# A graph network and expert kernel on one core: the transfers that clear the experts' input leave the first adjacency blocks and come at every fourth block from number 50 on

## The chip, the cores and the metric

The program runs on one core of a Trainium2 chip. The core has TensorE (PE in the rows), VectorE (DVE), ScalarE (ACT), GpSimd (POOL) and SyncE (SP). SyncE computes nothing here: it issues transfers, one after the other, in the order of its program, and waits in that order too. The metric is the device time of one execution in microseconds; lower is better.

## The reference, cut to what matters

A layer norm, four relational graph layers over 3125 nodes of width 256 and 100000 edges of four types, and a mixture of eight experts of which each node takes two:

```python
cnt = zeros((3125, 4)).at[dst, etype].add(1.0)
inv_deg = 1.0 / maximum(cnt[dst, etype], 1.0)
for l in range(4):
    h = einsum('ni,rio->rno', X, W[l])
    agg = segment_sum(h[etype, src] * inv_deg[:, None], dst)
    out = agg + X @ root[l] + bias[l]
    X = elu(layernorm(out) * gamma[l] + beta[l]) + X
...
top_vals, top_idx = top_k(xn @ Wr + br, 2);  w = softmax(top_vals)
y = sum over e of w_full[e] * (gelu(xn @ W1[e] + b1[e]) @ W2[e] + b2[e])
```

The edges are sorted by destination, and low destinations have many more edges than high ones.

## The kernel before, in words

The 3125 nodes are 25 tiles of 125. In layer 0 the first 12 tiles, numbered 0 to 11 ("dense" tiles), get an adjacency matrix: each tile is built in 25 blocks of five destination nodes, 300 blocks in all. A block is summed on TensorE (`pair`, L1859, from one-hot operands that VectorE makes at L1495 and L1500 and ScalarE at L1277 and L1280), and ScalarE copies it out (L1296). When a tile's 25 blocks stand, SyncE issues the tile's count row (L1145, a small transfer within the chip's memories called n_tabs<-n_BIG, on which TensorE's degree matmul L1833 waits) and the store of the whole tile to HBM, 3.1 MB (L1147, n_a<-n_BIG), to be read again in layers 1 to 3. The other 13 tiles ("far" tiles, 12 to 24) take their edges' rows by gathers that GpSimd issues (L1421), twelve of them ahead, and small matmuls (L1907); in layer 0 their edges are counted by L1845.

For each tile the counts become inverses on VectorE (L1515, L1517). They take a round trip: SyncE stores them (L1153, n_ind<-n_INVA, two transfers), waits for that store, and loads them back spread over all partitions (L1119, n_INVB<-n_ind). The end of a tile's sum (`finish`, L1601) multiplies by them and so waits for that load. Behind it come the transposes (L1772), the products with the layer's weights (L1923, L1927), and the norm on VectorE (L1627 and on).

The experts' input is a buffer n_xg in HBM of 25728 rows of 1028 bytes. It must be zero before the routing scatters rows into it, after layer 3. It is cleared by 54 transfers of 96 x 5 rows (L1212, n_xg<-n_tabs, the last one 96 x 3), 26.4 MB in all, issued by SyncE with no wait of their own but for the constants. Two places wait for all of them: the first ScalarE copy of layer 1's sums (L1309, step `fh` with i == T), which overwrites the zeros' source, and the first scatter (L1434).

One list, `order`, sets the work of all engines. `Near.steps` simulates the engines with fixed costs and appends steps; each engine's program walks the list and takes the steps that are its own. A `zx` step is one clearing transfer, and only SyncE takes it. `N_ZERO` is 54, `GPT` is 25 blocks to a tile. A second program for other inputs (`dense_scalar`, `dense_tensor` and more) stands behind a branch on a flag; with these inputs it is not taken, and the rows show none of its lines.

Of the kernel before, what the change touches and what calls it, by code (L numbers as in the profile page):

```python
# [24 lines left out]
GPT = TN // GD  # L25
# [19 lines left out]
BATCH = 4  # L45
# [4 lines left out]
ZROWS = 96  # L50
ZN = 5
N_ZERO = math.ceil((DUMMY + 128) / ZROWS / ZN)
ROWS = (0, 112), (112, TN)
HEAD = 32
SIGMA = 4.0
# [21 lines left out]
S8 = 8  # L77
# [42 lines left out]
class Near:  # L120
# [102 lines left out]
    def steps(self):  # L223


        TD, T_ = self.TD, T
        order = self.order = []
# [44 lines left out]
        def follow(what, l, n):  # L272
            if what == "wscale" and time["pe"] < begun[l]:
                later(time["pe"] + 0.5, what, l, n)
                return
            if what == "weights":
                load_weights(l)
                return
            if what in ROUTE:
                route(what, n)  # L280
                return
            order.append((what, l, n))
            if what == "post":
                at = run("dve", 4.1)
                posted[n] = at - 3.4
                later(at + 0.2, "exp", l, n)
            elif what == "exp":
                later(run("act", 0.45) + 0.5, "end", l, n)
            elif what == "end":
                at = run("dve", 1.2)  # L290
                t = self.done[n][1]
                if l + 1 < L:
                    later(at + 0.2, "high", l, n)
                else:
                    later(at + 0.3, "ra", l, n % T_)
            elif what == "high":
                later(run("act", 0.55) + 0.4, "low", l, n)
            elif what == "low":
                ended[l, self.done[n][1]] = run("dve", 0.5)
                later(time["dve"] + 0.2, "xstore", l, n)  # L300
            elif what == "split":
                later(run("dve", 1.3, run("act", 1.2)) + 0.4, "split_store", l, n)
                if n < 14:
                    order.append(("stage", l, n + 18))
                if n < 15:
                    later(time["pe"] + 24.0, "split", l, n + 1)
            elif what == "maxima":
                run("dve", 1.3)
                order.append(("stage", l, n + 2))
                if n < 15:  # L310
                    later(time["pe"] + 16.0, "maxima", l, n + 1)
                else:
                    job(time["dve"] + 0.2, "maximum", l, 0)
            elif what == "far":
                run("dve", 7.0)
                time["pe"] += 3.0
                far_ready[0] = time["dve"] + 4.0
                load_weights(0)
            elif what == "window":
                made[l, n] = run("dve", 0.65)  # L320
            elif what == "fh":
                if n and n - (1 if l == 0 else 2) not in products:
                    order.pop()
                    later(time["pe"] + 0.5, what, l, n)
                    return
                later(run("act", 1.1) + 0.2, "fl", l, n)
            elif what == "fl":
                sums[n] = run("dve", 1.2) + 0.2
                if n in turned:
                    job(max(sums[n], turned[n]), "product", l, n)  # L330
            elif what == "wmax":
                later(run("dve", 3.2) + 0.3, "wput", l, n)
            elif what == "wput":
                later(time["pe"] + 12.0, "wget", l, n)
            elif what == "wget":
                later(time["pe"] + 15.0, "wscale", l, n)
            elif what == "wscale":
                run("dve", 1.6)
                later(time["dve"] + 0.2, "wsplit", l, n)
            elif what == "wsplit":  # L340
                split_in[l] = run("dve", 3.0, run("act", 2.6)) + 0.3
            elif what == "block":
                unit_ready["block", n] = run("act", 0.6) + 0.2
                if n < N_ZERO:
                    order.append(("zx", 0, n))
            elif what == "tile":
                job(time["pe"] + 5.0, "degree", 0, n)
            elif what == "counts":
                counted[n] = run("act", 0.6) + 0.2
                job(counted[n], "degree", 0, n)  # L350
            elif what == "inverse":
                unit_ready["degree", n] = run("dve", 0.6) + 0.2
                later(time["dve"] + 0.2, "ind", 0, n)
            elif what == "ind":
                inverse[n] = time["pe"] + 2.5
                load_inverse(n)
# [170 lines left out]
        s = 0  # L527
# [2107 lines left out]
def dense_scalar(e, a, c, m, s):  # L2635
    TD = c.TD
# [9 lines left out]
    for i in range(0, 2 * c.PT, 4):  # L2646
        n = 128 * min(4, 2 * c.PT - i)
# [7 lines left out]
    e.sem_inc(s["evac"], 4)  # L2655
    e.wait_ge(s["eg"], 32)
    e.wait_ge(s["prep"], c.prep["gp_sub"])
    regs = [e.alloc_register(f"er{TD}_{i}") for i in range(BATCH)]
    for t in range(TD):
        if t >= 2:  # L2660
            e.wait_ge(s[f"store{t % 2}"], 16 * (t // 2))
        rows = m.RA[:, 5 * (t % 2):5 * (t % 2) + 5, :].rearrange("p a b -> p (a b)").rearrange(
            "p (k q) -> p k q", q=W)
        for i in range(GPT):
            if i % BATCH == 0:
                n = min(BATCH, GPT - i)
                e.reg_load(regs[0:n], m.egrow[0:1, GPT * t + i:GPT * t + i + n])
            e.wait_ge(s["slot_free"], e.snap(regs[i % BATCH], min_val=1, max_val=c.P) + S8)
            e.activation(rows[:, :, 20 * i:20 * i + 20], m.bank((GPT * t + i) % 4, 0, W).rearrange(
                "p (q k) -> p k q", k=T), ACT.Copy).then_inc(s["evac"], 1)  # L2670

    for what, l, i in c.order:
# [14 lines left out]
        elif what == "end" and l + 1 < L:  # L2687
            t = c.done[i][1]
# [5 lines left out]
        elif what == "split":  # L2694
            n = 512 if i < E8 else 256
# [7 lines left out]
        elif what == "xo" or (what == "ra" and i + 2 < T):  # L2703
            n = i if what == "xo" else i + 2
# [371 lines left out]
def dense_tensor(e, a, c, m, s):  # L3076
    TD = c.TD
# [12 lines left out]
    e.wait_ge(s["tab"], 32)  # L3090
    e.wait_ge(s["vs"], math.ceil(c.PT / 2))
    e.wait_ge(s["prep"], c.prep["b1t"])
    regs = [e.alloc_register(f"pr{TD}_{i}") for i in range(3 * BATCH)]
    n_os = 0
    for p0 in range(0, c.P, BATCH):
        n = min(BATCH, c.P - p0)
        for w in range(3):
            at = w * c.PT * 128 + p0
            e.reg_load(regs[BATCH * w:BATCH * w + n], m.tabrow[0:1, at:at + n])
        for i in range(n):  # L3100
# [3 lines left out]
            if p % 2 == 0:  # L3104
                n_os += (p % 14 in OSG) + ((p + 1) % 14 in OSG and p + 1 < c.P)
                e.wait_ge(s["oc"], min(p + 2, c.P))
                e.wait_ge(s["os"], n_os) if n_os else None
                last = 2 * BATCH + min(i + 1, n - 1)
                e.wait_ge(s["evac"], e.snap(regs[last], min_val=1, max_val=c.G + 1))
            e.matmul(m.PS[:, bass.ds(clear, 2)], m.OS[:, p % S8, :], m.Z[:, :], start=True, stop=False,  # L3110
                     skip_group_check=True)
            e.matmul(m.PS[:, bass.ds(at, W)], m.OS[:, p % S8, :], m.OC[:, p % S8, :], start=False, stop=False,
# [171 lines left out]
```

## Time and profile before

| | us |
|---|---|
| median of 3 runs | 2614.72 |
| lowest, highest | 2608.05, 2615.36 |
| profiled execution: span from first to last instruction | 2581.8 |
| median less span | 32.9 |

The profiled execution's time is known by its span alone; what lies around it is taken as the 32.9 us between the span and the median of the runs. In the span TensorE is busy 2075.7 us (80%), VectorE 1572.2 us (61%), GpSimd 1253.4 us (49%), ScalarE 818.3 us (32%). Layer 0 ends near 868 us, layers 1 to 3 fill the time to about 2340 us, and the experts the rest. In a timeline row the first number is the start in us from the span's start, the second the time from the first to the last of the merged instructions; the bracket is the engine's idle time just before and what ended it.

### The profile page before, as it was taken

What the parts mean: (1) busy time and instruction counts of PE and PEld (TensorE: products, weight loads), DVE (VectorE), ACT (ScalarE), POOL (GpSimd) and SP (SyncE); (2) the same over time, 40 slices, a digit from 0 to 9 for tenths busy, and PEclk for the clock granted to TensorE, in tenths of its full rate; (3) what the DMA queues carried; (4) which work ended last, traced back from release to release, by engine and by line L of the source; (5) the groups of instructions that cost most, each with busy time, mean ns of one, the idle gap of its engine ahead of it and who ended that gap; (6) DMA issues with size and microseconds to landing.
All of it is one profiled execution on the core that took longest, in us unless ns stands there. A gap on an engine that the chain in (4) does not pass through costs nothing. (4 is left out here: it accounts for less than half of the span.)

```text
span 2581.8 us, 46238 instructions
## 1 busy us (share of the span) xinstructions
PE 2075.7 (80%) x16327; PEld 1296.1 (50%) x16327; DVE 1572.2 (61%) x4475; ACT 818.3 (32%) x1674; POOL 1253.4 (49%) x1223
## 2 busy tenths in 40 slices
PE   0576788787879889898889888898987988774992
PEld 0334455454545455555545545454554645454992
DVE  5976677575656356566553656566364766575665
ACT  1564556454456011111111212111011111123992
POOL 2124333544430266666716666662665656752441
PEclk9988899988889899899989999999997999986996
DMA  5698333444432487666637867765775655532335
GB/s 144 187 273 256 115 112 115 133 123 125 122 112 98 145 256 233 219 210 210 187 113 249 257 210 240 236 218 158 230 231 165 181 163 169 179 101 64 95 94 178
DMA packets 211755, 445.56 MB, mean 173 GB/s; under 512 B 40819, under 2 KB 137088, under 8 KB 209733
## 3 DMA queue, kind: packets, MB, share of 16 engines
q1 hardware_dynamic: 138357, 274.65, 34.6%
q0 software_dynamic: 61408, 156.79, 20.1%
q10 hardware_dynamic: 11760, 11.08, 1.7%
q8 instruction: 141, 2.31, 0.4%
q14 instruction: 89, 0.73, 0.1%
HBM read 338.14 MB, written 103.90 MB: 171 GB/s over the span
## 5 line engine op out<-in xcount | busy, mean ns | idle before, releaser
L1421 POOL DMA_INDIRECT n_BIG<-n_xd,n_SIDX x1080 | 1110.9, 1029 | 1091.2 <-PE n_PS L1907 501.3
L1888 PE MATMUL n_PS<-n_BIG 125*128 125x500 f16 x4800 | 1196.8, 388 | 69.3 <-issue 45.3
L1888 PEld LDWEIGHTS n_PS<-n_BIG 125*128 125x128 f16 x4800 | 441.1, 100 | 508.7 <-issue 142.0
L1907 PEld LDWEIGHTS n_PS<-n_OW,n_BIG 128*128 128x128 f16 x4320 | 256.3, 99 | 204.6 <-issue 68.9
L1907 PE MATMUL n_PS<-n_OW,n_BIG 128*128 128x84 f16 (+21 forms) x4320 | 303.5, 201 | 51.5 <-issue 41.6
L1927 PE MATMUL n_PS<-n_BIG,n_tabs 128*128 128x256 f16 x2400 | 299.3, 280 | 19.4 <-issue 18.9
L1601 DVE TENSOR_TENSOR n_ST<-n_PS,n_INVB 128x500 f32<-128x500 f32 x200 | 199.9, 1041 | 158.4 <-issue 47.6
L1927 PEld LDWEIGHTS n_PS<-n_BIG,n_tabs 128*128 128x128 f16 x2400 | 239.7, 101 | 62.9 <-issue 29.0
L1627 DVE SCALAR_TENSOR_TENSOR n_U<-n_PS,n_cw,n_BI 125x256 f32<-125x256 f32 x100 | 48.2, 482 | 334.9 <-PE n_PS L1927 161.3
L1296 ACT ACTIVATE n_BIG<-n_PS 128x500 f16<-128x500 f32 x300 | 164.3, 578 | 195.5 <-PE n_PS L1859 93.6
L1312 ACT ACTIVATE n_tabs<-n_ST 128x1000 f16<-128x1000 f32 x100 | 103.8, 1038 | 358.8 <-DVE n_ST L1601 192.3
L1508 DVE TENSOR_TENSOR n_OW<-n_io,n_tabs 128x460 f16<-128x460 f16 (+14 forms) x216 | 140.8, 657 | 119.4 <-PE n_PS L1907 59.7
L1323 ACT ACTIVATE n_U<-n_U 125x256 f32<-125x256 f32 x100 | 41.4, 414 | 506.6 <-issue 268.3
L1859 PE MATMUL n_PS<-n_BIG,n_tabs 128*128 128x500 bf16 (+4 forms) x590 | 140.8, 346 | 66.3 <-ACT n_BIG L1296 25.8
L1495 DVE TENSOR_SCALAR n_BIG<-n_io,n_tabs 128x500 bf16<-128x500 f16 (+4 forms) x590 | 154.4, 312 | 63.5 <-PE n_PS L1859 59.9
L1523 DVE TENSOR_TENSOR n_tabs<-n_ST,n_tabs 128x1000 f16<-128x1000 f32 x100 | 120.1, 1201 | 45.2 <-ACT n_tabs L1312 25.9
L1303 ACT ACTIVATE n_XT<-n_PS 128x500 f16<-128x500 f16 x100 | 58.7, 587 | 257.3 <-remote 139.8
L1441 POOL DMA_INDIRECT n_yg<-n_BIG,n_IDX x56 | 64.3, 1148 | 113.7 <-DVE n_BIG L2083 113.1
L1923 PE MATMUL n_PS<-n_RL,n_XT 128*128 128x256 f16 x600 | 88.5, 286 | 38.3 <-issue 21.5
L1277 ACT ACTIVATE n_tabs<-n_io,n_tabs 128x125 bf16<-128x125 f16 x294 | 93.2, 390 | 74.4 <-PE n_PS L1859 69.5
L1859 PEld LDWEIGHTS n_PS<-n_BIG,n_tabs 128*128 128x128 bf16 x590 | 56.8, 104 | 112.5 <-issue 38.0
L1923 PEld LDWEIGHTS n_PS<-n_RL,n_XT 128*128 128x128 f16 x600 | 57.6, 101 | 60.2 <-issue 24.2
(271 smaller groups left out, 2252.9 us busy)
## 6 DMA issues: line engine op xcount, KB each, us to landing
n_BIG<-n_a SPq DMA_DIRECT2D x175, 625.0 KB
n_a<-n_BIG SPq DMA_DIRECT2D x12, 3125.0 KB
n_xg<-n_tabs SPq DMA_DIRECT2D x53, 481.9 KB
n_INVB<-n_ind SPq DMA_DIRECT2D x100, 250.0 KB
n_BIG<-n_xd,n_SIDX POOLq DMA_INDIRECT x1080
n_BIG<-in_L_ffn_W_dram SPq DMA_DIRECT2D x32, 512.0 KB
n_xd<-n_BIG SPq DMA_DIRECT2D x75, 112.0 KB
n_whl<-n_BIG SPq DMA_DIRECT2D x16, 512.0 KB
```

Of the source, the lines that this page charges most:

```text
L1296: e.activation(rows[:, :, 20 * g:20 * g + 20], m.bank(4 + c.unit_of["block", i], 0, W).rearrange("p (q k) -> p k q", k=T), ACT.Copy).then_ ...
L1312: e.activation(m.SH[i % 2 if l else 0][:, 0, :, :, 0:TN], m.ST, ACT.Copy).then_inc(s["shi"], 1)
L1421: e.indirect_dma_start(m.GR[:, g % GS, :], None, m.XD[l % 2][:, :], bass.IndirectOffsetOnAxis(ap=m.SIDX[:, i:i + 1], axis=0)).then_inc(s[f ...
L1495: e.tensor_scalar(m.OC[i % S][:, at], m.io[:, at], m.VS[:, i:i + 1], None, ALU.is_equal).then_inc(s["oc"], 1)
L1508: e.tensor_tensor(m.OW[:, i % OW_, 0:n * wide].rearrange("p (c w) -> p c w", w=wide), m.io[:, 0:wide].unsqueeze(1).broadcast_to([128, n, w ...
L1523: e.tensor_tensor(lo, m.ST, hi, ALU.subtract).then_inc(s["slo"], 1)
L1601: ins = e.tensor_tensor(m.ST[:, h], m.bank(2 * p + h, 0, W).rearrange("p (n r) -> p r n", r=R), m.INVB[:, k, :].rearrange("p (n r) -> p r ...
L1859: e.matmul(m.bank(4 + c.unit_of["block", g])[:, at], m.OS[b % 3][:, i % 4, :], m.OC[i % S][:, at], start=(j == 0), stop=(j + 1 == c.groups ...
L1888: ins = e.matmul(m.bank(2 * p + h, 0, W), m.xps[l % 2][0:TN, part, D * k + 128 * h:D * k + 128 * h + 128], m.RA[0:TN, c.slot_of(n), W * (k ...
L1907: ins = e.matmul(m.bank(2 * p + h, at, c.width[q]), m.GR[:, g % GS, D * part + 128 * h:D * part + 128 * h + 128], ow, start=(first == 0 an ...
L1923: e.matmul(out, m.XT[:, f % 2, 2 * x + h, :], m.RH[:, l % 2, w, h, :], start=(x + w + h == 0), stop=False)
L1927: ins = e.matmul(out, sums[:, x, h, r, :], m.WH[:, l % 2, w, h, r, :], start=False, stop=(x == 1 and h == 1 and r == R - 1))
```

## The change: what it does

The step list gets its `zx` steps at other places. Before, the step follows each of blocks 0 to 53. Now it follows blocks 50, 54, 58 and so on to 262, the same 54 transfers. In the words of the change these begin at tile 1's last adjacency block; by the number in the code block 50 is the first block of tile 2, the one after tile 1's last.

```diff
+ZERO_FROM, ZERO_STEP = 50, 4
...
             elif what == "block":
                 unit_ready["block", n] = run("act", 0.6) + 0.2
-                if n < N_ZERO:
-                    order.append(("zx", 0, n))
+                if n >= ZERO_FROM and (n - ZERO_FROM) % ZERO_STEP == 0 and (n - ZERO_FROM) // ZERO_STEP < N_ZERO:
+                    order.append(("zx", 0, (n - ZERO_FROM) // ZERO_STEP))
```

The second program, behind the branch, changes too: it reads each wait's bound from a table in on-chip memory as it comes, not four at a time.

```diff
-    regs = [e.alloc_register(f"er{TD}_{i}") for i in range(BATCH)]
...
-            if i % BATCH == 0:
-                n = min(BATCH, GPT - i)
-                e.reg_load(regs[0:n], m.egrow[0:1, GPT * t + i:GPT * t + i + n])
-            e.wait_ge(s["slot_free"], e.snap(regs[i % BATCH], min_val=1, max_val=c.P) + S8)
+            at = GPT * t + i
+            e.wait_ge(s["slot_free"], e.value_load(m.egrow[0:1, at:at + 1], min_val=1, max_val=c.P) + S8)
...
-    regs = [e.alloc_register(f"pr{TD}_{i}") for i in range(3 * BATCH)]
+    regs = [e.alloc_register(f"pr{TD}_{i}") for i in range(2 * BATCH)]
...
-                last = 2 * BATCH + min(i + 1, n - 1)
-                e.wait_ge(s["evac"], e.snap(regs[last], min_val=1, max_val=c.G + 1))
+                last = 2 * c.PT * 128 + p0 + min(i + 1, n - 1)
+                e.wait_ge(s["evac"], e.value_load(m.tabrow[0:1, last:last + 1], min_val=1, max_val=c.G + 1))
```

What SyncE is given, from the count row and store of tile 0 to the count row of tile 1. Here n_ind<-n_INVA stores the inverses, n_INVB<-n_ind loads them back, n_xg<-n_tabs clears. Before:

```order
L1145 DMA n_tabs<-n_BIG 25x1x500
L1147 DMA n_a<-n_BIG 128x12500
L1212 DMA n_xg<-n_tabs 96x5x514 x3
L1153 DMA n_ind<-n_INVA 112x4
L1153 DMA n_ind<-n_INVA 13x4
L1119 DMA n_INVB<-n_ind 128x500
L1212 DMA n_xg<-n_tabs 96x5x514 x14
L1153 DMA n_ind<-n_INVA 112x4
L1153 DMA n_ind<-n_INVA 13x4
L1119 DMA n_INVB<-n_ind 128x500
L1212 DMA n_xg<-n_tabs 96x5x514 x8
L1145 DMA n_tabs<-n_BIG 25x1x500
```

The same stretch of SyncE's program in the changed kernel, up to the first of the inverses behind tile 1's store:

```order
L1146 DMA n_tabs<-n_BIG 25x1x500
L1148 DMA n_a<-n_BIG 128x12500
L1154 DMA n_ind<-n_INVA 112x4
L1154 DMA n_ind<-n_INVA 13x4
L1120 DMA n_INVB<-n_ind 128x500
L1154 DMA n_ind<-n_INVA 112x4
L1154 DMA n_ind<-n_INVA 13x4
L1120 DMA n_INVB<-n_ind 128x500
L1146 DMA n_tabs<-n_BIG 25x1x500
L1148 DMA n_a<-n_BIG 128x12500
L1213 DMA n_xg<-n_tabs 96x5x514 x2
L1154 DMA n_ind<-n_INVA 112x4
```

The 25 clearing transfers between the two tiles' rows are gone, the 21 ahead of tile 0's row as well, and two stand behind tile 1's store where four stood.

SyncE's program from the count row of tile 6 to the load of inverses behind it, before:

```order
L1145 DMA n_tabs<-n_BIG 25x1x500
L1147 DMA n_a<-n_BIG 128x12500
L1172 DMA n_xd<-n_BIG 224x1x256
L1172 DMA n_xd<-n_BIG 26x1x256
L1153 DMA n_ind<-n_INVA 112x4
L1153 DMA n_ind<-n_INVA 13x4
L1119 DMA n_INVB<-n_ind 128x500
```

The same place in the changed kernel:

```order
L1146 DMA n_tabs<-n_BIG 25x1x500
L1148 DMA n_a<-n_BIG 128x12500
L1213 DMA n_xg<-n_tabs 96x5x514
L1173 DMA n_xd<-n_BIG 224x1x256
L1173 DMA n_xd<-n_BIG 26x1x256
L1154 DMA n_ind<-n_INVA 112x4
L1154 DMA n_ind<-n_INVA 13x4
L1120 DMA n_INVB<-n_ind 128x500
```

One clearing transfer now stands between the tile's store and the round trip of the inverses. No other engine's instructions in the taken program move.

## Rows read from the trace of the kernel before

**Rows 1.** Windows: length, busy PE, PEld, DVE, ACT, POOL, PE clock, DMA share, GB/s.

```profile
89.00:250.00 161.00, 106.89 (x712) 61.93 (x711) 118.63 (x402) 89.55 (x204) 55.55 (x53) 0.88 0.90 259
250.00:400.00 150.00, 123.67 (x893) 72.27 (x891) 101.95 (x325) 88.72 (x202) 55.26 (x54) 0.92 0.38 112
```

**Rows 2.** TensorE's waits from 150 to 230 us: us, times, longest.

```profile
PE n_PS L1772 <- DVE n_ST L1601: 10.1, 1, 10.1
PE n_PS L1833 <- DMA n_tabs<-n_BIG: 5.6, 1, 5.6
```

**Rows 3.** SyncE's timeline from 85 to 330 us.

```profile
89.09 11.56 SPq L1212 DMA_DIRECT2D n_xg<-n_tabs  x7
...
152.38 0.87 SPq L1145 DMA_DIRECT2D n_tabs<-n_BIG  x1
...
175.25 27.67 SPq L1212 DMA_DIRECT2D n_xg<-n_tabs  x14
203.43 3.19 SPq L1153 DMA_DIRECT2D n_ind<-n_INVA  x2
212.19 0.34 SPq L1119 DMA_DIRECT2D n_INVB<-n_ind  x1
...
233.90 11.86 SPq L1212 DMA_DIRECT2D n_xg<-n_tabs  x4
247.24 2.31 SPq L1153 DMA_DIRECT2D n_ind<-n_INVA  x2
255.19 0.34 SPq L1119 DMA_DIRECT2D n_INVB<-n_ind  x1
...
324.00 0.79 SPq L1153 DMA_DIRECT2D n_ind<-n_INVA  x2
325.73 0.35 SPq L1119 DMA_DIRECT2D n_INVB<-n_ind  x1
```

**Rows 4.** VectorE's timeline around the ends of tiles.

```profile
196.34 0.18 DVE L1517 RECIPROCAL n_INVA<-n_INVA 125x4 f32<-125x4 f32 x1
...
206.69 1.20 DVE L1523 TENSOR_TENSOR n_tabs<-n_ST,n_tabs 128x1000 f16<-128x1000 f32 x1
215.79 1.96 DVE L1601 TENSOR_TENSOR n_ST<-n_PS,n_INVB 128x500 f32<-128x500 f32 x2 [7.89 <-DMA n_INVB<-n_ind]
...
264.97 1.96 DVE L1601 TENSOR_TENSOR n_ST<-n_PS,n_INVB 128x500 f32<-128x500 f32 x2 [3.74 <-DMA n_INVB<-n_ind]
```

**Rows 5.** TensorE and SyncE at a quiet count row, from 790 to 797 us.

```profile
792.10 0.73 SPq L1145 DMA_DIRECT2D n_tabs<-n_BIG  x1
...
795.35 0.59 PE L1833 MATMUL n_PS<-n_ON,n_tabs 25*125 25x1 f16 x4 [1.62 <-DMA n_tabs<-n_BIG]
```

**Rows 6.** TensorE's timeline from 155 us: a dense step at two clocks.

```profile
158.92 0.59 PE L1833 MATMUL n_PS<-n_ON,n_tabs 25*125 25x1 f16 x4 [5.62 <-DMA n_tabs<-n_BIG]
159.59 5.76 PE L1888 MATMUL n_PS<-n_BIG 125*128 125x500 f16 x16
...
166.46 1.01 PE L1888 MATMUL n_PS<-n_BIG 125*128 125x500 f16 x4
```

**Rows 7.** SyncE behind tile 6's store, from 553 to 574 us.

```profile
559.52 2.81 SPq L1153 DMA_DIRECT2D n_ind<-n_INVA  x2
568.28 0.35 SPq L1119 DMA_DIRECT2D n_INVB<-n_ind  x1
```

**Rows 8.** VectorE at two later ends of tiles.

```profile
440.23 2.03 DVE L1601 TENSOR_TENSOR n_ST<-n_PS,n_INVB 128x500 f32<-128x500 f32 x2
...
571.57 2.02 DVE L1601 TENSOR_TENSOR n_ST<-n_PS,n_INVB 128x500 f32<-128x500 f32 x2 [0.65 <-DMA n_INVB<-n_ind]
```

**Rows 9.** SyncE at tile 4's round trip and behind tile 9's store.

```profile
435.66 0.35 SPq L1119 DMA_DIRECT2D n_INVB<-n_ind  x1
...
756.55 0.35 SPq L1119 DMA_DIRECT2D n_INVB<-n_ind  x1
```

**Rows 10.** TensorE's waits from 250 to 860 us with no releaser in the profile.

```profile
PE n_PS L1907 <- issue: 8.9, 10, 1.2
```

More of the change, by code:

```diff
@@ L3096, in dense_tensor @@
         n = min(BATCH, c.P - p0)
-        for w in range(3):
+        for w in range(2):
             at = w * c.PT * 128 + p0
```

## The prediction
> **What bounds the kernel now.** I read the windows of layer 0 first, because the change moves nothing outside it. From 89 to 250 us, where the 54 clearing transfers are issued, TensorE is busy 106.89 of 161 us (66%) at a DMA share of 0.90; in the next 150 us it is busy 123.67 (82%) at a share of 0.38 [rows 1]. So the stretch that the change relieves is the one where TensorE is least busy and the DMA engines nearly full. That alone is no gain: the first tiles are slow also since VectorE builds one-hot operands for many edges, and it is busy 118.63 us there. What counts is which wait ends last. In TensorE's waits between 150 and 230 us the two longest hang on transfers: 10.1 us for VectorE's finish, and 5.6 us for the count row [rows 2]. The first needs VectorE's timeline: the finish at 215.79 had itself sat idle 7.89 us for the load of the inverses [rows 4]. SyncE's timeline tells why that load was late. The inverses stood at 196.34 + 0.18 = 196.52, but SyncE was in a group of 14 clearing transfers from 175.25 to 202.92, issued their store at 203.43, saw it landed only at 212.19 and issued the load then [rows 3]. Fourteen in 27.67 us is 1.98 us each: the queue is full, and SyncE issues at the speed at which it drains.
>
> The engines hold fixed orders, and no later stage starts at a fixed time. Time lost by VectorE and TensorE together in this stretch shifts everything behind it, and time won does the same.
>
> **Part 1, the count row of tile 0.** SyncE issued it at 152.38, and TensorE's degree matmul started at 158.92, 6.54 us later, after 5.62 us idle [rows 3, 6]. The same pair late in the layer, with no clearing about: issued 792.10, used 795.35 after an idle of 1.62, so 3.25 us [rows 5]. After the change nothing clears ahead of tile 0, and I take the quiet latency: 6.54 - 3.25 = **3.3 us** off. Of the 5.6 us wait 2.3 stay. Bounds: 0, if the other traffic holds it up as much, and 5.6, the whole wait.
>
> **Part 2, the inverses of tile 12.** In a quiet place the store was issued at 324.00 and the load at 325.73, 1.73 us later, against 8.76 us here (203.43 to 212.19) [rows 3]. The load took 215.79 - 212.19 = 3.60 us under traffic, and I keep that as the upper bound for the quiet one. So the inverses would be there at 196.5 + 1.7 + 3.6 = 201.8, before VectorE ends its work ahead of the finish at 206.69 + 1.20 = 207.89 [rows 4]. The wait goes whole: **7.9 us**. What is late next is VectorE's own work, then TensorE's transposes, which would still idle 10.1 - 7.9 = 2.2 us. Bounds: 3 us, if only SyncE's 6.9 us of lateness went and half of it were taken up elsewhere, and 7.9.
>
> **Part 3, the inverses behind tile 1's store.** The third finish waits 3.74 us at 264.97 [rows 4]. Its store of inverses was issued at 247.24 and the load at 255.19, 7.95 us against 1.73 in the quiet place, behind tile 1's store (3.1 MB) and four clearing transfers, which came behind eight more [rows 3]. After the change the store of the tile stays and two clearing transfers follow it. Two instead of twelve take 10 x 1.98 = 19.8 us of transfer time out of the queue before that point, five times the wait. I take it whole, **3.7 us**; bounds 0 and 3.74.
>
> **Part 4, the clock.** After the 5.62 us idle TensorE ran 16 dense matmuls in 5.76 us, and later four in 1.01, so 16 would take 4.04: 1.7 us lost at the lower granted clock [rows 6]. The wait there gets shorter but does not vanish, and the one of part 2 falls from 10.1 to 2.2. I take **1 us**; bounds 0 and 3.4, the same loss twice.
>
> **Part 5, what the 54 transfers cost where they come to stand.** They have no wait of their own, so they start when SyncE gets past the waits ahead of them, in clumps of one to five, from tile 1's store (233 us) to the load at 756.55 [rows 3, 9]. That is 54 x 1.98 = 107 us of full queue spread over 523 us, where the DMA share is near 0.38 [rows 1]: there is room, if nothing urgent stands behind a clump. The urgent ones are the round trips of inverses. Behind tile 6's store the round trip already takes 8.76 us (559.52 to 568.28), and its finish waits 0.65 us [rows 7, 8]. One clearing transfer now stands ahead of it: +1.98 us, all of it on the path. At tile 4 the load was issued at 435.66 and the finish began at 440.23, 4.57 us later, against 3.6 for a load; the slack is 1.0 us, so one more transfer costs 1.98 - 0.97 = 1.0 us [rows 8, 9]. Behind the other stores no finish shows a wait for this load, and I count nothing. Sum **3 us**. Gathers: TensorE's unexplained waits at the far matmuls are 8.9 us over 610 us [rows 10]; a queue fuller by a fifth adds about **1 us**. Bounds of this part: 0, and the rival below. The two steps that wait for all 54 (layer 1's first copy, near 868 us, and the scatter) come over 100 us after the last is issued: nothing. The changes in the second program stand behind a branch not taken: nothing.
>
> In the Trainium skill, "DMA: Bandwidth & Descriptors", section on queues, rings and completion order, each DMA engine takes its turns between the queue rows by packets, and consumes one row's descriptors in ring order. The trace agrees with the second half (the store of inverses took 8.76 us behind the clump and 1.73 without). The same page, in the section that issuing engines are not separate DMA queues, says that DMAs of different issuing engines run on the same 16 DMA engines and interleave, which speaks against the change: by it the clearing takes the gathers' time wherever it stands, and part 5's last term would be nearer that of rival A.
>
> **Sum.** -3.3 - 7.9 - 3.7 - 1.0 + 3.0 + 1.0 = -11.9 us on the span of 2581.8, so 2569.9; with the 32.9 us between span and median, 2602.8. **I forecast 2603 us.**
>
> **Rivals.** *A, the clearing lands on the urgent transfers (slower).* Between a tile's store and the next round trip stands one transfer at each of tiles 4 to 8 and two at tiles 1 and 9, nine in all. If each costs its 1.98 us, that is 18 us, and if in addition one clearing transfer in five delays a gather on which TensorE waits, 11 x 1.98 = 22 us more; less the 15.9 us won, +24: 2639. It decides from a cost of 16 us on. For it: the queue is in order, and gathers run twelve ahead with waits already in rows 10. Against: SyncE mostly sits in long waits when it meets a clump, so the clump is gone before the next urgent one; and a gather twelve ahead has twelve chunks of work for cover.
> *B, the gain is taken up (no change).* TensorE is short of operands from VectorE all through this stretch; removing 7.9 us of idle on both helps only if neither had stored work in it. If half of parts 1 to 3 is lost, 7.5 + 1 - 4 = -4.5: 2610. For it: VectorE's one-hot work is limited to twelve ahead, so it cannot run ahead, which is also what speaks against: both engines truly stopped.
> *C, more comes back.* At a DMA share of 0.90 every gather is slow as well, and the restart of the far matmuls after 224 us waits for fresh ones; with all waits on transfers gone (5.6 + 7.9 + 3.7), 3.4 for the clock and no cost, -20.6: 2594.
> *D, the clearing does not move in time.* It would have to be issued elsewhere than the list says; the order of SyncE's program shows it moved. Gain 0.
>
> **Chances.** Forecast 0.45, C 0.17, B 0.23, A 0.12, D 0.03. A measurement of this kernel tells about 0.3% (7.8 us) from no change, so faster means below 2606.9. The forecast's own spread (2598 to 2608) puts most of it there; with C that is 0.60 faster. B, D and the rest of the forecast, 0.29 same. A, 0.11 slower. The range for 8 in 10 runs from 2591 to 2617: down to C, up past B, and into the small end of A.
>
> **What would show it.** Right: in the windows TensorE's busy share from 89 to 250 us rises to about 72%, the DMA share falls to near 0.5, the finish after 206 us has no idle for n_INVB, SyncE's store and load of inverses are 2 us apart near 197 us, SyncE's first clearing transfer stands behind tile 1's store near 222 us, where 233.90 began the last four, and layer 0 ends 10 to 14 us earlier; from there on the traces run parallel. The degree matmul still waits about 2 us. Wrong: a new wait of VectorE for n_INVB longer than 3 us behind one of the stores of tiles 4 to 9, or far matmuls waiting more than 15 us in sum. Then the cost in part 5 was too small.

## The result, and the profile after

The changed kernel takes 2594.31 us (median of 6 runs, 2590.3 to 2604.16), against 2614.31 us of the kernel before (6 runs). The ratio on record is 0.9943, 95% interval 0.9918 to 0.9967. Two further timings of the same change, below, gave 0.9949 and 0.9931. The mean of the three is 0.9941, so 15 us of 2614. The plain quotients of the medians lie lower, at 0.9923, 0.9945 and 0.9927 with a mean of 0.9932 (18 us); the text goes by the ratios on record. One execution of after_again took 2986.85 us at a granted clock of 0.698, where all others had 0.90 to 0.93, and no ratio counts it. The forecast of 2603 us is a ratio of 0.9955: faster, as forecast, and inside the range. That 2594.31 is also rival C's 2594 is luck: by the ratio the gain is 15 us, not C's 20.6.

The windows of layer 0, in the order of [rows 1]:

```profile
89.00:250.00 161.00, 119.91 (x783) 68.56 (x783) 125.22 (x420) 96.59 (x222) 61.72 (x60) 0.85 0.40 117
250.00:400.00 150.00, 125.84 (x923) 74.73 (x924) 105.11 (x339) 87.56 (x201) 60.53 (x59) 0.94 0.54 160
```

In the first stretch TensorE's busy share rose from 66% to 74%, the share of the DMA engines fell from 0.90 to 0.40, and all four engines ran more instructions (TensorE 783 instead of 712). The share of the second stretch rose from 0.38 to 0.54, where the clearing went.

TensorE's longest waits from 150 to 230 us, as in [rows 2]:

```profile
PE n_PS L1860 <- ACT n_BIG L1297: 12.6, 6, 6.3
PE n_PS L1773 <- DVE n_ST L1602: 2.4, 1, 2.4
PE n_PS L1860 <- issue: 1.6, 3, 1.1
```

The wait for VectorE's finish fell from 10.1 to 2.4 us, and the one for the count row is gone. In their place TensorE waits 12.6 us for ScalarE's copies of the adjacency blocks, of which the same stretch of before had 3.6. So part of what it gained it spends waiting for a helper.

SyncE's timeline, for [rows 3]:

```profile
151.22 0.87 SPq L1146 DMA_DIRECT2D n_tabs<-n_BIG  x1
152.14 0.43 SPq L1148 DMA_DIRECT2D n_a<-n_BIG  x1
...
190.79 0.75 SPq L1154 DMA_DIRECT2D n_ind<-n_INVA  x2
193.06 0.34 SPq L1120 DMA_DIRECT2D n_INVB<-n_ind  x1
220.54 0.73 SPq L1146 DMA_DIRECT2D n_tabs<-n_BIG  x1
221.31 0.44 SPq L1148 DMA_DIRECT2D n_a<-n_BIG  x1
221.80 1.73 SPq L1213 DMA_DIRECT2D n_xg<-n_tabs  x2
234.57 0.84 SPq L1154 DMA_DIRECT2D n_ind<-n_INVA  x2
240.61 0.35 SPq L1120 DMA_DIRECT2D n_INVB<-n_ind  x1
```

Tile 12's inverses go out at 190.79 and are asked back at 193.06, 2.27 us apart, where it was 8.76. The first clearing transfer stands at 221.80, behind tile 1's store.

VectorE's inverses of tile 12 and the three finishes, for [rows 4]:

```profile
190.58 0.18 DVE L1518 RECIPROCAL n_INVA<-n_INVA 125x4 f32<-125x4 f32 x1
197.96 1.99 DVE L1602 TENSOR_TENSOR n_ST<-n_PS,n_INVB 128x500 f32<-128x500 f32 x2
201.05 1.20 DVE L1524 TENSOR_TENSOR n_tabs<-n_ST,n_tabs 128x1000 f16<-128x1000 f32 x1
202.39 1.99 DVE L1602 TENSOR_TENSOR n_ST<-n_PS,n_INVB 128x500 f32<-128x500 f32 x2
...
251.15 2.02 DVE L1602 TENSOR_TENSOR n_ST<-n_PS,n_INVB 128x500 f32<-128x500 f32 x2
```

None of these three finishes has an idle time for n_INVB any more; later in layer 0 VectorE still waits 3.9 us for it, in three. The one that stood at 215.79 starts at 202.39.

TensorE at tile 0's degree matmul, for [rows 6]:

```profile
155.23 0.62 PE L1834 MATMUL n_PS<-n_ON,n_tabs 25*125 25x1 f16 x4
155.78 0.26 PE L1860 MATMUL n_PS<-n_BIG,n_tabs 128*128 128x200 bf16 x1
155.88 3.54 PE L1889 MATMUL n_PS<-n_BIG 125*128 125x500 f16 x16
```

There is no wait, and the 16 dense matmuls behind it take 3.54 us, where they took 5.76.

One execution is not enough to say how much layer 0 gained, because events of equal kernels lie up to 4 us apart. SyncE's issue of a tile's store is an event that every kernel has. The table gives its time for two kernels with the old places and three with the new (they come from the runs below):

| store of tile | 0 | 1 | 2 | 3 | 5 | 7 | 9 | 11 |
|---|---|---|---|---|---|---|---|---|
| before | 153.30 | 233.40 | 303.51 | 365.27 | 485.18 | 613.27 | 744.77 | 835.22 |
| early_places | 154.43 | 236.68 | 304.05 | 365.38 | 487.40 | 615.15 | 743.54 | 835.69 |
| after | 152.14 | 221.31 | 286.14 | 347.49 | 471.36 | 602.18 | 729.36 | 821.70 |
| after_again | 150.42 | 220.16 | 285.16 | 345.43 | 469.97 | 603.64 | 733.43 | 825.64 |
| after_third | 149.76 | 221.52 | 285.99 | 347.62 | 473.44 | 603.45 | 733.40 | 823.20 |
| mean new less mean old | -3.1 | -14.0 | -18.0 | -18.5 | -14.7 | -11.1 | -12.1 | -11.9 |

18 us are won by tile 3, 7 of them are lost again by tile 7, and 12 us are left at the end of layer 0.

The column of tile 0 does not show faster work. The row and the store of a tile wait for ScalarE's copy of its 25th block, and in before that copy ended at 149.19, while SyncE stood in four clearing transfers until 152.33 and issued the row at 152.38:

```profile
148.15 1.04 ACT L1296 ACTIVATE n_BIG<-n_PS 128x500 f16<-128x500 f32 x2
```

```profile
146.56 5.77 SPq L1212 DMA_DIRECT2D n_xg<-n_tabs  x4
```

The same copy ended at 149.36 in early_places, with the row at 153.50, and at 151.20, 149.47 and 148.81 in the three changed kernels, with the row 0.02 to 0.03 us behind it. So SyncE itself came 3.2 and 4.1 us late to the row with the old places.

### The profile page after: what moved, and what is told of

It reads as the page before. It is cut to its first block and busy times, and to the rows that moved or that the text cites. A ratio compares the mean times of both kernels' runs of the same rounds, so it can differ in the third digit from the quotient of the medians.

```text
span 2601.5 us, 46238 instructions
## 1 busy us (share of the span) xinstructions
PE 2092.8 (80%) x16327; PEld 1297.5 (50%) x16327; DVE 1572.7 (60%) x4475; ACT 817.9 (31%) x1674; POOL 1251.7 (48%) x1223
## 3 DMA queue, kind: packets, MB, share of 16 engines
q0 software_dynamic: 61408, 156.79, 20.6%
## 5 line engine op out<-in xcount | busy, mean ns | idle before, releaser
L1928 PE MATMUL n_PS<-n_BIG,n_tabs 128*128 128x256 f16 x2400 | 309.4, 284 | 35.1 <-issue 33.4
## 6 DMA issues: line engine op xcount, KB each, us to landing
n_xg<-n_tabs SPq DMA_DIRECT2D x53, 481.9 KB
```

What stands on the lines that cost most here:

```text
L1928: ins = e.matmul(out, sums[:, x, h, r, :], m.WH[:, l % 2, w, h, r, :], start=False, stop=(x == 1 and h == 1 and r == R - 1))
```

## The experiments

Theory 1: the time comes from the transfers on which an engine waits (the count row, the round trips of inverses), which stood behind full queues. Rivals: it comes from the gathers, slowed by plain traffic (theory 2 below); or from something else that the edit changed. A second question is what the 54 transfers cost at their new places.

### The old places, and the change again: early_places, after_again

```diff
-ZERO_FROM, ZERO_STEP = 50, 4
+ZERO_FROM, ZERO_STEP = 0, 1      # early_places
```

> The changed kernel with its clearing transfers back at blocks 0 to 53, so that only the second, untaken program differs from the kernel before. My measure beside the time is when SyncE issues tile 11's store, the last of layer 0: 835.2 us before, 821.7 us in the changed kernel. Theory (the untaken program costs and brings nothing): store at 835 +- 1, time within 0.3% of before. Rival (a part of the gain comes from the other program, by its code's size or place): store at 828 or less and a time 8 us or more under before.

> The changed kernel again, for a second trace and more times. Both theories: store of tile 11 at 822 +- 2, time 12 to 20 us under before. If the span's stretch behind layer 0 differs by more than 5 us from the first trace of the same kernel, what the first two traces show there (the changed kernel losing 25 us from 1600 us on) is spread between executions and not the change.

Measured: early_places 2611.61 us, ratio 1.0012 (0.9991 to 1.0032); after_again 2595.07 us (median of all 12 executions), ratio 0.9949 (0.9922 to 0.9976). With the old places VectorE waits 11.3 us for n_INVB (longest 7.0) and TensorE 5.7 for the count row, as in before. Tile 11's store stands at 835.69, where 835 +- 1 was expected and the rival had 828. So the untaken second program has no effect that can be measured, and the places alone are the change.

### The wait of tile 12 alone: round_trip_first

Old places, but the 14 transfers that stood ahead of tile 12's inverses come behind their load.

```diff
+        held = [x for x in self.order if x[0] == "zx" and 28 <= x[2] < 42]
+        order = [x for x in self.order if x not in held]
+        at = order.index(("inv", 0, self.TD)) + 1
+        self.order = order[:at] + held + order[at:]
```

> As early_places, but the 14 clearing transfers that SyncE issued between the two round trips of inverses come behind the load of tile 12's inverses. The bytes up to tile 1's store stay the same. Theory (SyncE's order is what costs: the store of inverses sits behind the clump): the finish that waited 7.89 us waits under 2, store of tile 11 at 828, time 7 us under before. Rival (the full DMA engines cost, not the order): the wait stays above 5 us, store at 833 or later, time as before.

Measured: 2624.63 us, ratio 1.0057 (1.0035 to 1.0080), 0.6% slower; tile 11's store at 849.77, where the theory had 828 and the rival 833 or later. SyncE's timeline:

```profile
198.96 0.75 SPq L1162 DMA_DIRECT2D n_ind<-n_INVA  x2
200.91 0.34 SPq L1128 DMA_DIRECT2D n_INVB<-n_ind  x1
201.29 39.89 SPq L1221 DMA_DIRECT2D n_xg<-n_tabs  x22
241.23 0.74 SPq L1154 DMA_DIRECT2D n_tabs<-n_BIG  x1
242.01 0.82 SPq L1156 DMA_DIRECT2D n_a<-n_BIG  x1
```

The round trip is 1.95 us and its wait of 7 us is gone, which is half of theory 1. (VectorE's only wait for n_INVB in this layer is 3.5 us at 274.94.) But SyncE, freed early, went straight into 22 clearing transfers and was in them for 39.89 us. Tile 1's count row came only behind them, and TensorE waited for it:

```profile
PE n_PS L1842 <- DMA n_tabs<-n_BIG: 18.9, 3, 13.0
```

That wait of 13.0 us was not there before. So here the transfers cost through SyncE itself: while its queue is full it stands, and everything later in its program stands with it. Taking one wait away moved the cost to the next urgent transfer. By this run the gain of the change needs the stretch to be cleared as a whole.

### The new start with the old density: from50_step1

```diff
-ZERO_FROM, ZERO_STEP = 50, 4
+ZERO_FROM, ZERO_STEP = 50, 1
```

> The changed kernel with the transfers at each of blocks 50 to 103, four times as dense. Theory (clearing costs where it stands ahead of an urgent round trip or store; density raises that): the first 230 us as in the changed kernel (tile 1's store at 221), then 6 to 12 us lost over tiles 2 and 3, store of tile 11 at 830, time 5 us under before. Rival (only the first two tiles are sensitive, anywhere later is free): store at 822, time as the changed kernel.

Measured: 2612.16 us, ratio 1.0015 (0.9990 to 1.0039): no gain is left. The window of tiles 2 and 3, SyncE in it, and the finish that stands for its wait:

```profile
250.00:400.00 150.00, 111.91 (x785) 64.72 (x782) 91.32 (x292) 77.02 (x175) 47.75 (x47) 0.92 0.86 256
```

```profile
297.73 23.79 SPq L1213 DMA_DIRECT2D n_xg<-n_tabs  x9
321.62 2.58 SPq L1154 DMA_DIRECT2D n_ind<-n_INVA  x2
330.08 0.35 SPq L1120 DMA_DIRECT2D n_INVB<-n_ind  x1
```

```profile
333.52 1.97 DVE L1602 TENSOR_TENSOR n_ST<-n_PS,n_INVB 128x500 f32<-128x500 f32 x2 [12.17 <-DMA n_INVB<-n_ind]
```

The picture of before stands 100 us later: DMA share 0.86, a clump, a round trip of 8.46 us, a wait of 12.17. Tile 3's store comes at 366.24, where after_again has 345.43: 20.8 us lost, twice what was expected, and as much as the change wins. So the spacing by four is as needed as the later start.

### Out of layer 0 altogether: layers_1_and_2

The first transfer stays at block 50; the other 53 copy its zeros within HBM, at the stores of activations in layers 1 and 2 (each moves its bytes twice, a read and a write of HBM).

```diff
+            if x[0] == "xstore" and x[1] >= 1:
+                for _ in range(2 if x[1] == 1 else 1):
+                    if n < N_ZERO:
+                        order.append(("zx", 1, n))
```

> No clearing in layer 0 but the first transfer; the other 53 copy its 480 zero rows within HBM, two behind each xstore step of layer 1 and one behind those of layer 2. It bounds what clearing costs in layer 0 at all. Theory (at the changed kernel's places it costs about 4 us): tile 11's store at 818, 4 us before the changed kernel's 822. Rival (it costs 8 us and more there, and the slow loss from tile 2 to tile 11 in both traces of the changed kernel is that cost): store at 813 or less. If the loss over tiles 2 to 11 against a kernel with early clearing shows here too, it is the clock's and not the transfers'. Time: layer 0's gain less what 53 transfers cost in layers 1 and 2, where the DMA share is 0.65 to 0.7: between the changed kernel and 10 us slower.

Measured: 2597.74 us, ratio 0.9981 (0.9956 to 1.0006). In layer 0 VectorE's waits for n_INVB are 0.3 us in all, and tile 11's store comes at 819.54, 4 us ahead of the mean of the three runs of the change, which is as far as these lie from each other. The timed ratio is the worse by 0.4% (0.9981 against 0.9941, with intervals that overlap). In layers 1 and 2 the copies meet a stretch that was fuller than layer 0:

```profile
870.00:1600.00 730.00, 637.35 (x4839) 374.35 (x4838) 400.91 (x959) 107.43 (x160) 440.08 (x430) 0.96 0.84 246
```

The same window of after_again:

```profile
870.00:1600.00 730.00, 643.76 (x4871) 378.08 (x4872) 408.65 (x975) 113.12 (x167) 446.63 (x435) 0.95 0.70 212
```

TensorE is 6.4 us less busy in it. So layer 0 looks like the better place, and by this run its 54 transfers cost about 4 us there. The loss between tiles 3 and 7 shows in this kernel too, without any clearing in it; the expectation would have laid that to the clock, and the granted clocks given under part 5 below do not bear this out.

### Number or bytes: early_fifth

54 transfers of 96 rows each at the old places, and the other four fifths of the bytes in 54 at the new ones.

```diff
+            late, i = i >= 100, i % 100
...
+            row, n = (row + ZROWS, n - 1) if late else (row, 1)
```

> All 54 instructions stand at blocks 0 to 53 again but clear a fifth each (96 rows), and the other four fifths of each come at the changed kernel's places: 108 transfers. Theory (what costs is bytes that stand in SyncE's queue, not the number of instructions): SyncE issues each in 0.5 us or less, no finish waits over 2 us before tile 1's store, that store at 222 to 225, tile 11's at 822 to 826, time 10 us or more under before. Rival (54 more instructions in SyncE's order cost as such): tile 1's store at 230 or later.

Measured: 2596.16 us, ratio 0.9957 (0.9932 to 0.9982); VectorE's waits for n_INVB 7.2 us in three, longest 3.7; TensorE's for the count row 1.6; tile 1's store at 224.39 (means 235.0 and 221.0 of the table). 54 issues early with a fifth of the bytes bring back 3.4 of the 14 us, about a fifth. It is the bytes that cost before tile 1's store, and not the number of issues. Tile 11's store missed the expected 822 to 826: it came at 832.68, which this run does not explain.

### Another engine issues the early ones: gpsimd_30_early

GpSimd issues 30 of them before its first gather, SyncE the other 24 from block 50 at every ninth.

```diff
+    for i in range(ZERO_POOL):
+        clear(e, m, s, i)
     e.wait_ge(s["vs"], math.ceil(c.PT / 2))
```

> GpSimd issues 30 of the transfers before its first gather, on its own queue, and SyncE the other 24 at every ninth block from 50. The DMA engines are as full as before until about 135 us, but SyncE's order is free. Theory (the place in SyncE's order costs, not full engines): tile 0's store at 152, tile 1's at 221 to 224, tile 11's at 818 to 822, time as the changed kernel or up to 4 us under. Rival (full engines cost whoever issues): the weights and first gathers are late, tile 1's store at 230 or later, time 5 us or more above the changed kernel. In the Trainium skill, DMA: Bandwidth & Descriptors, section Queues, rings and completion order, each DMA engine takes turns between queue rows; by that rule the theory's outcome is the one to expect.

Measured: 2623.32 us, ratio 1.0079 (1.0051 to 1.0106), 0.8% slower, and tile 1's store at 248.20: the rival's outcome, against the theory. GpSimd's row and then SyncE's:

```profile
67.18 22.45 POOL L1249 DMA_DIRECT2D n_xg<-n_tabs  x30 [17.77 <-issue]
```

```profile
76.72 68.49 SPq L1138 DMA_DIRECT2D n_xd<-n_BIG  x4
145.25 2.40 SPq L1085 DMA_DIRECT2D n_BIG<-in_L_gnn_weights_dram  x2
```

After_again, with no clearing there:

```profile
76.82 12.52 SPq L1138 DMA_DIRECT2D n_xd<-n_BIG  x4
111.05 0.96 SPq L1085 DMA_DIRECT2D n_BIG<-in_L_gnn_weights_dram  x2
```

GpSimd got rid of its 30 in 22 us. But SyncE's four stores of rows, issued at the same time, took 68.49 us instead of 12.52, and the weights behind them came 34 us late:

```profile
155.75 2.88 DVE L1540 TENSOR_REDUCE n_wm<-n_BIG 128x1 f32<-128x2048 f32 x2 [28.98 <-DMA n_BE<-in_L_gnn_ln_beta_dram]
```

The queues' packets, bytes and share of the 16 DMA engines' time in this kernel from 67 to 145 us (q0 is GpSimd's, q1 SyncE's):

```profile
q0 software_dynamic: 4320, 14.81, 69.1%
q1 hardware_dynamic: 5871, 2.98, 14.9%
```

So a second engine's queue does not hide the bytes from the first: the engines gave 69.1% of their time to GpSimd's bytes and SyncE's 2.98 MB had to do with 14.9%. That agrees with the Trainium skill, "DMA: Bandwidth & Descriptors", in the section that issuing engines are not separate DMA queues: all of them run on the same 16 DMA engines. The expectation had leaned on taking turns instead. By packets the two queues did come near each other (4320 and 5871), but from the bytes above a packet of GpSimd's held 3.4 KB and one of SyncE's 0.5 KB on average.

### Early, where nothing urgent follows: early18_clear_of_stores

The trace of before has two places where the queue may fill: blocks 0 to 17, where SyncE next waits for work of VectorE, and the time behind a load of inverses. 18 transfers go to the first, 36 to every sixth block from 50, and none stands between a tile's store and the next load of inverses. (The inverses of two tiles often follow one store. The transfers held back then stand between the first load and the second round trip.)

```diff
+                if n < ZERO_EARLY or (n >= ZERO_FROM and (n - ZERO_FROM) % ZERO_STEP == 0):
...
+                behind = (x[0] == "tile" or behind) and x[0] != "inv"
+            while held and not behind and n < N_ZERO:
+                order.append(("zx", 0, n))
```

> 18 transfers at blocks 0 to 17, where no transfer is urgent before 151 us, and 36 at every sixth block from 50, none between a tile's store and the load of inverses behind it. Theory (only transfers ahead of an urgent one cost): no finish waits over 1 us for its inverses in layer 0, tile 1's store at 221 to 223, tile 11's at 818 to 820, time 2 to 5 us under the changed kernel. Rival (any clearing before 151 us costs, through the weights or the count row): tile 0's store late by 2 us or more, and the time as the changed kernel or above.

Measured: 2583.33 us, ratio 0.9921 (0.9896 to 0.9946). Here the kernel before had 2606.26, so the ratio is what compares. The first 18 are in the queue from 88.89 to 135 us, and tile 0's count row comes at 148.69, no later than without them. VectorE's waits for n_INVB are 1.0 us in all. From 89 to 150 us the DMA share is 0.82 here and 0.25 in the changed kernel, and TensorE's degree matmul starts at 154.38 against 155.23: in this stretch the fuller DMA engines alone cost nothing.

### Which half of that, and is it real: after_third, clear_of_stores, early18_only, early18_again

Four kernels on one chip, a two-by-two of "18 early" and "none behind a store".

> The changed kernel once more, as the corner of a two-by-two with the next three: 54 clearing transfers at every fourth block from 50, some of them between a tile's store and the next load of inverses. Both earlier timings lay at 0.994 to 0.995 of the kernel before, so 0.995 +- 0.003. Layer 0's last store of a tile (tile 11) starts within 4 us of 823.

> As the changed kernel, but each clearing transfer whose place lies between a tile's store and the next load of inverses waits until behind that load; none stands ahead of block 50. If what the changed kernel gives back in tiles 3 to 11 is the load of inverses held up behind clearing transfers (theory 1), VectorE's waits for n_INVB fall to about 1 us in layer 0, and tile 11's store starts 3 to 5 us sooner than in the changed kernel; the time is 0.2% less, ratio about 0.993. If it is the plain traffic beside the gathers (theory 2), the same 54 transfers cost the same and the ratio is the changed kernel's within 0.001.

> 18 of the 54 transfers stand at blocks 0 to 17, where neither the row of tile 0 nor a load of inverses stands behind them, and 36 at every sixth block from 50, with no care for the stores. By theory 1 the places behind stores are still used, by fewer: a third of the gain of the next kernel over the changed one, ratio about 0.994. By theory 2 the later traffic is thinner by a third, and the whole of the next kernel's gain shows here, ratio about 0.992.

> Both edits, 18 early and none between a store and a load of inverses: the fastest so far, once more, on the same chip as the changed kernel. Its earlier ratio to the kernel before was 0.9921. If its lead is real it lies 0.2 to 0.3% (5 to 8 us) below the changed kernel of this same call, with tile 11's store 4 to 7 us sooner; if the earlier lead was the spread between chips, within 0.1% of it.

| | ratio to before | 95% | waits for n_INVB | tile 11's store |
|---|---|---|---|---|
| after_third | 0.9931 | 0.9913 to 0.9949 | 3.7 us | 823.20 |
| clear_of_stores | 0.9927 | 0.9912 to 0.9942 | 6.4 us | 829.22 |
| early18_only | 0.9921 | 0.9906 to 0.9936 | 2.3 us | 821.77 |
| early18_again | 0.9915 | 0.9895 to 0.9935 | 1.3 us | 817.97 |

Neither half does what theory 1 wanted of it: clear_of_stores is the changed kernel's equal where 0.2% was expected, and early18_only alone has the whole of the lead (0.9921), which was theory 2's outcome. All four intervals overlap, so the times do not decide. Keeping clear of the stores does not take the waits away either, but the longest of the four, 3.9 us, is of the edit's own making. It is the third finish, and SyncE's rows ahead of it are:

```profile
238.27 0.96 SPq L1229 DMA_DIRECT2D n_xg<-n_tabs  x2
239.27 3.74 SPq L1189 DMA_DIRECT2D n_xd<-n_BIG  x2
243.10 1.21 SPq L1170 DMA_DIRECT2D n_ind<-n_INVA  x2
248.31 0.35 SPq L1136 DMA_DIRECT2D n_INVB<-n_ind  x1
```

The two clearing transfers moved from behind tile 1's store to behind the first load, and so ahead of the second round trip, whose load this finish awaits. In the changed kernel, with nothing there, the same rows' stores (n_xd) take 1.6 to 2.1 us and the trip 3.0 to 4.2 in three profiles; here 3.74 and 5.21. So clear_of_stores is no clean test of theory 1.

What the edit does at tile 6 can be read. The round trip with no clearing ahead of it takes 7.85 us all the same:

```profile
548.27 3.09 SPq L1170 DMA_DIRECT2D n_ind<-n_INVA  x2
556.12 0.35 SPq L1136 DMA_DIRECT2D n_INVB<-n_ind  x1
```

In the changed kernel one stands there, and it takes 9.10 us; in before, with none, 8.76 [rows 7].

```profile
542.42 1.96 SPq L1213 DMA_DIRECT2D n_xg<-n_tabs  x1
545.39 2.24 SPq L1173 DMA_DIRECT2D n_xd<-n_BIG  x2
547.73 3.06 SPq L1154 DMA_DIRECT2D n_ind<-n_INVA  x2
556.83 0.35 SPq L1120 DMA_DIRECT2D n_INVB<-n_ind  x1
```

So most of this round trip's length is there without clearing, presumably from the tile's own store of 3.1 MB; no run shows that apart. The trip alone hides what the transfer costs, since SyncE also starts it later. From the tile's store to the load of the inverses behind it, over all 14 profiles, it shows (us, and the number of kernels):

| tile | no clearing between | one transfer | two |
|---|---|---|---|
| 4 | 12.9 to 14.3 (10) | 15.6 to 15.8 (4) | |
| 6 | 13.2 to 13.9 (8) | 14.9 to 16.0 (6) | |
| 9 | 11.3 to 12.3 (9) | 14.1 (1) | 15.2 to 16.3 (4) |

By the means a clearing transfer makes this load 1.7 to 2.1 us later. At tile 6 VectorE then waits 1.93, 1.31 and 2.07 us in the three changed kernels, against 0.65 and 0.77 with the old places and 0.72 in clear_of_stores.

The 18 early ones are the better half by both ratios (0.9921 and 0.9915 against 0.9931 and 0.9927), but 0.1% lies inside the intervals. early18_again is the lowest in every column, and against the changed kernel timed beside it, it has 2597.14 us to 2599.15, 2 us and not the 5 to 8 expected. In both profiles of this kernel layer 0 is shorter, by 5.4 us in the mean (818.28 and 817.97 against the changed kernel's 823.5). I take it as slightly better; its lead over the changed kernel is not settled.

## Why the prediction was right, and where it was not

**Part 1, the count row: too small.** Forecast -3.3 us with 2.3 us of wait left. The degree matmul came 3.7 us sooner (158.92 to 155.23), 4.0 us behind the issue of the row. The whole wait of 5.62 went, but TensorE came to this matmul some 2 us later than in before. The repeats do not have that lateness: over the two kernels with the old places and the three with the new the matmul comes 4.9 us sooner (158.92 and 160.82 against 155.23, 155.19 and 154.53). What the forecast left out is that SyncE's issue of the row was late as well, by 3.2 us, and not only its landing.

**Part 2, tile 12's inverses: right.** Forecast -7.9. The reciprocal of tile 12 came 5.8 us sooner (196.34 to 190.58) and the finish behind it 13.4 (215.79 to 202.39): 7.6 between the two. The finish began as soon as VectorE's work ahead of it ended (202.25), and TensorE's transposes still waited 2.4 us, forecast 2.2. round_trip_first shows that this wait is removed by taking the clump from ahead of the store alone, and that this does not suffice.

**Part 3, the third finish: right in size, read from the wrong load.** The wait of 3.74 is gone in two of three profiles of the change and 0.77 in after_again. The prediction laid it to the load issued at 255.19, but the finish at 264.97 comes 9.8 us behind that one and 3.5 behind the next, which fits the 3.60 of part 2:

```profile
258.20 0.89 SPq L1153 DMA_DIRECT2D n_ind<-n_INVA  x2
261.48 0.35 SPq L1119 DMA_DIRECT2D n_INVB<-n_ind  x1
```

These inverses stood at 250.13, and SyncE, waiting for the first round trip of 7.95 us, stored them 8 us later. The cause is the same, one step further along SyncE's program.

**Part 4, the clock: the local loss came back, and more than was booked.** The 16 matmuls took 2.2 us less (5.76 and 5.86 against 3.54 in all three), where the forecast saw 1.7 at that place and booked 1 in all. The granted clock over them was 0.61 in before, after the wait of 5.62 us, and 1.00 in the changed kernel. The mean granted clock of 89 to 250 us did not rise, however: 0.88 in before, 0.85 after. In equal kernels it is 0.77 (early_places) and 0.82 (after_again), so a mean over 161 us says nothing of a change of this size.

**The sum of parts 1 to 4** was -15.9 us. By tile 3 the difference of the means is -18.5. Parts 1 and 4 are 1.6 and 1.2 us short of what came, which is about the 2.6 us between. The 3.1 us ahead of tile 0's store are SyncE's lateness with the row, and belong to part 1: nothing ahead of it ran faster, though the DMA share from 89 to 153 us fell from 0.91 in before. So the gain needs none of rival C's slow gathers.

**Part 5, what the transfers cost: the round trips right, the total too small.** At tiles 4 and 6 one transfer makes the load 2.1 and 1.7 us later, near the 1.98 of the forecast. Of that not all becomes a wait: behind tile 3 VectorE waits 3.9, 3.7 and 2.1 us for n_INVB in the three changed kernels, against 0.65 and 0.77 with the old places, so 2.5 us more where 3 were booked. For the gathers 1 us was booked, and none came: TensorE's waits without a releaser at the far matmuls are 7.0, 5.8 and 8.9 us against 8.9 and 9.4. Yet 7 us were given back between tiles 3 and 7, where the forecast had 4 for the whole layer and said that the traces would run parallel. This total is the term that was mis-sized. Gains of 15.9 and costs of 4 were booked, 18.5 and 6.6 came, and that both give -11.9 is luck. Is the clearing what takes the 7 us? From tile 3's store to tile 11's, against the clearing transfers issued between them:

| kernel | us | clearing |
|---|---|---|
| before, early_places | 470.0, 470.3 | 0 |
| layers_1_and_2, round_trip_first | 477.7, 478.4 | 0 |
| from50_step1 | 478.5 | 4 |
| gpsimd_30_early | 477.2 | 18 |
| early18_clear_of_stores, early18_again, early18_only | 471.6, 472.3, 480.1 | 27 |
| after, after_third, after_again | 474.2, 475.6, 480.2 | 41 |
| clear_of_stores, early_fifth | 480.8, 481.1 | 41 |

Two kernels with no clearing there take 478 us as well, and one with 27 takes 471.6. So most of what is given back is not the traffic, as rival A and my part 5 had it. Nor is it the clock: from tile 3's store to tile 7's the granted clock is 0.93 and 0.91 with the old places, 0.92, 0.92 and 0.91 in the changed kernels and 0.92 in layers_1_and_2, and TensorE is busy 210 to 214 us in all six. It is idle there for 38.0 and 35.8 us with the old places and for 41.8 to 44.5 in the four others, spread over many short waits. Perhaps the order meets this stretch with other offsets between the engines than in before; equal kernels differ by 6 us in it. What it is in detail stays open: I have no run that holds the offsets and changes the traffic only.

**The base: wrong, without effect on the forecast.** I took 32.9 us as lying around the span. It is 1.9: the profiled execution of the changed kernel took 2603.38 us with a span of 2601.5, and all others show the same. The one profiled execution of before was simply a quick one. Behind tile 11's store it needs 1746.6 us, while the 13 others need 1761.0 to 1779.8 (for the same program, but for the copies of layers_1_and_2). So the span rises by 20 us from before to after although the kernel is 15 us faster. The sum was made against the span and then led back to the median by the same 32.9 us, which cancels. Anyone who compared the two spans would have called the change slower.

**The rivals.** A (the clearing lands on urgent transfers) is real as a mechanism: from50_step1 shows it at 20.8 us in a clump, and at every fourth block it makes loads late by about the 1.98 us a transfer that A had, of which 2.5 us become waits and not 18. B (the gain is taken up) holds for none of the first three parts. C had gains of 20.6 us, near the 18.5 that came, though not by faster gathers, and no cost. D is excluded by the timeline.

## What to carry to other kernels

Here background transfers cost mostly by what stood behind them in the issuing engine's program: look for the next transfer on which an engine waits, and let the queue fill only where that engine has a long wait of its own before it. Space them out instead of moving them as a block (the same 54 at a new place without spacing gave no gain). Before you count a wait as the whole cost, look whether the transfer behind it was itself issued late, as the count row was. Do not hand them to another engine's queue at a time when urgent bytes move. A single wait taken away may bring the next one: here it turned 7 us into 13. And a gain counted from waits need not reach the end of the stage: 7 of 18 us were lost again, for a reason that stays open.

## What the runs showed of the hardware

- A full queue stops the issuing engine, not only its transfers: SyncE passed 22 transfers of 481.9 KB in 39.89 us, 1.81 us each (round_trip_first), and 2 in 1.73 us at 221.80, behind nothing but the tile's store (after).
- GpSimd's queue took 30 transfers of the same size in 22.45 us, 0.75 us each, but SyncE's four stores of rows, issued at the same time, then took 68.49 us instead of 12.52.
- A small store, its wait and the issue of its load take 1.7 to 2.3 us with little traffic. At tile 6, begun 5 to 6 us behind a 3.1 MB store, they take 7.7 to 8.8 us with no clearing transfer between (8 kernels) and 8.5 to 10.1 with one (6). Each clearing transfer between the tile's store and the load makes the load 1.7 to 2.1 us later (tiles 4, 6 and 9).
- From 89 to 150 us a DMA share of 0.82 to 0.86 instead of 0.25 (the three kernels with 18 early against the changed one) did not delay TensorE's degree matmul: 154.0 to 154.9 against 154.5 to 155.2.
- One profiled execution of this program lay 14 to 33 us from the others behind the same point. Distances between like events inside one stage, over several kernels, told differences of 4 us and more.
